# Latent attention with its scores computed twice: row maxima first, then probabilities as keys x queries

## What is computed

```python
x = x + _attn_ref(_layernorm(x), W_dq, W_uq, W_dkv, W_uk, W_uv, W_o)
# inside: nh = 16 heads of hs = 8
c_kv = x @ W_dkv.T
q = x @ W_dq.T @ W_uq.T
q_lat = einsum('bqhd,hdl->bhql', q, k_eff)
attn = einsum('bhql,bkl->bhqk', q_lat, c_kv) / sqrt(hs)
attn = softmax(where(causal, attn, -inf), axis=-1)
y_lat = einsum('bhqk,bkl->bhql', attn, c_kv)
y = einsum('bhql,hld->bqhd', y_lat, v_eff)
```

## Time and profile before

| | |
|---|---|
| median of 3 runs | 2167.96 us |
| the profiled execution's own time | 2170.55 us |
| its span, first to last instruction | 2168.7 us |
| mean granted TensorE clock | 0.955 of 2.4 GHz |
| TensorE (PE) busy | 1785.8 us, 82% |
| its weight loads (PEld) busy | 1079.9 us, 50% |
| DVE (VectorE) busy | 1488.3 us, 69% |
| ACT (ScalarE) busy | 1112.0 us, 51% |
| POOL (GpSimd) busy | 905.7 us, 42% |
| attention stage, first score to last addition | 882.4 to 1341.4 us |

### The profile page before, as it was taken

One profiled execution on the slowest core, in us unless ns is written; L12 is line 12 of the kernel. 1 busy time (PEld: TensorE's weight loads), 2 busy tenths in 40 slices (PEclk: granted clock), 3 DMA queues, 4 the chain that ended last, 5 costly groups with the idle time before them and its releaser, 6 DMA issues. The chain is left out here.

```text
span 2168.7 us, 50695 instructions
## 1 busy us (share of the span) xinstructions
PE 1785.8 (82%) x20074; PEld 1079.9 (50%) x20074; DVE 1488.3 (69%) x2281; ACT 1112.0 (51%) x2070; POOL 905.7 (42%) x624
## 2 busy tenths in 40 slices
PE   1578888888888886899999997578888888888885
PEld 1344444555555543566666664344454455555543
DVE  2567777677666753688888886567777677766752
ACT  1134444454544542688888886234444454544542
POOL 2445544555445540332233321445544555445530
PEclk9889999999999998899999998689999999999998
DMA  4234434544455441000000000334344544355441
GB/s 140 37 58 71 69 62 76 77 80 69 71 79 81 73 68 36 1 1 2 1 2 1 2 1 1 37 63 72 63 71 70 81 75 74 66 85 84 84 72 40
DMA packets 66076, 119.03 MB, mean 55 GB/s; under 512 B 13183, under 2 KB 23603, under 8 KB 63667
## 3 DMA queue, kind: packets, MB, share of 16 engines
q1 hardware_dynamic: 65843, 115.79, 31.8%
HBM read 49.55 MB, written 3.28 MB: 24 GB/s over the span
## 5 line engine op out<-in xcount | busy, mean ns | idle before, releaser
L786 DVE SCALAR_TENSOR_TENSOR TP<-bank,cols,tab 128x1024 f32<-128x1024 f32 x256 | 318.4, 1274 | 51.5 <-PE bank L450 42.5
L946 POOL TENSOR_TENSOR QK<-QK,RB 128x1024 f32<-128x1024 f32 x128 | 302.4, 2363 | 118.6 <-DMA RB<-RN 118.6
L940 POOL TENSOR_TENSOR QK<-TP 128x512 f32<-128x512 f32 x128 | 164.9, 1289 | 327.4 <-DVE TP L786 291.3
L1205 ACT ACTIVATE PL<-bank,NM 128x384 f32<-128x384 f32 (+3 forms) x512 | 255.7, 539 | 15.8 <-DVE NM L1286 13.0
L1286 DVE TENSOR_REDUCE NM<-bank 128x1 f32<-128x384 f32 (+3 forms) x352 | 217.9, 635 | 35.6 <-PE bank L1119 31.7
L809 DVE TRANSPOSE_TENSOR_REDUCE MX<-bank 128x16 f32<-128x512 f32 x256 | 160.2, 681 | 118.3 <-PE bank L487 118.3
L642 ACT ACTIVATE SQ<-bank 128x512 f32<-128x512 f32 x128 | 76.5, 598 | 275.7 <-PE bank L450 275.5
L1128 PE MATMUL bank<-cst,PL 128*128 128x128 f32 x1280 | 199.7, 275 | 3.6 <-DVE PTL L1295 1.4
L827 DVE TENSOR_TENSOR OT<-bank,OT 128x512 f32<-128x512 f32 x128 | 85.3, 687 | 160.9 <-DMA OT<-sums_d 146.9
L1114 PE MATMUL bank<-KL,QZL 128*128 128x384 f32 (+3 forms) x512 | 189.8, 422 | 2.3 <-DVE QZL L1242 2.3
L648 ACT ACTIVATE SQ<-bank 128x512 f32<-128x512 f32 x128 | 76.5, 598 | 201.2 <-DVE TP L786 201.2
(11 more groups left out here) (169 smaller groups left out, 3655.8 us busy)
## 6 DMA issues: line engine op xcount, KB each, us to landing
RB<-RN SPq DMA_DIRECT2D x512, 64.0 KB, 4.0
OT<-sums_d SPq DMA_DIRECT2D x128, 256.0 KB, 4.0
V<-V SPq DMA_DIRECT2D x32, 512.0 KB, 6.0
V<-V SPq DMA_DIRECT2D x32, 384.0 KB, 7.1
RB<-vars_d SPq DMA_DIRECT2D x32, 256.0 KB, 3.2
X<-in_L_attn_x SPq DMA_DIRECT2D x8, 256.0 KB, 4.6
out<-X SPq DMA_DIRECT2D x8, 256.0 KB, 4.7
wqkv_raw<-in_L_ffn_wqkv SPq DMA_DIRECT2D x1, 1536.0 KB
```

Of the source, the lines that this page charges most:

```text
L786: nc.vector.scalar_tensor_tensor(out=TP[:, o:o + 2, :], in0=BK[4 + z][:, :].unsqueeze(1).to_broadcast([P, 2, T]), scalar=q, in1=tab[:, e, ...
L940: nc.gpsimd.tensor_tensor(QK[:, m, 0, :], TP[:, 2, :], TP[:, 1, :], ALU.subtract)
L946: nc.gpsimd.tensor_tensor(QK[:, m, :, :], QK[:, m, :, :], RB[:, m, :].unsqueeze(1).to_broadcast([P, 2, T]), ALU.mult).then_inc(S["nr_ok"], 1)
L1205: last = nc.scalar.activation(PL[:, m % PRING, h * N:(h + 1) * N], BK[m % SRING][:, h * N:(h + 1) * N], ACT.Exp, bias=NM[:, m % SRING, h:h ...
```

## The change

It touches the attention stage and, in the setup, the layout of folded weights and constants. A group now has 6 units in place of 11, each a pair of heads in a pair of banks (1024 columns): `FILLS` puts query block 3 in the first, blocks 2 and 0 in the second, block 1 in the third; two units each, for the two pairs of heads. Every head has 32 rows of its own: 8 high, 8 low and again 8 values, a row (24) for the maximum, and zeros; for the two heads of a pair the products use different 32-row strips.

Per step m TensorE issues the first pass for unit m: masks, then scores, queries x keys (`scores`). DVE takes maxima over both banks (`maxima`). When a group is through, TensorE turns the maxima (`turn_max`, 4 transpositions into bank 7) and DVE adds them to the queries' row 24 (`add_max`), against which the keys have a one. Eight steps later the second pass computes keys x queries with the maximum already in it, and the masks behind it (`scores_t`); ACT takes one exp over both banks straight into `PTL` (`softmax_exp`). PV then needs no transposed copy; it comes in three steps, with key blocks 1 and 3 together. The output copy goes to ACT, the splitting of queries and keys to POOL, and queries and keys are prepared two groups ahead. Both passes share a ring of three bank pairs; the turned output goes back into bank 6.

```diff
-                PT_LAG, PV_LAG, YT_LAG = 3, 5, 11
-                EV_LAG, OT_LAG, Y_LAG = 3, 8, 11
-                SRING, PRING = 4, 4
-                B_PT, B_O, B_PREP = (4, 5), 6, 7
+                FILLS = [((3, 0),), ((2, 0), (0, 3 * P)), ((1, 0),)]
+                DIAG = [(3 * P, T), (2 * P, T), (P, 2 * P)]
+                FILLS_T = [((0, 0),), ((3, 0), (1, P)), ((2, 0),)]
+                DIAG_T = [(0, P), (0, 2 * P), (0, P)]
+                WIDTH_T = [T, T, 2 * P]
+                UN = 2 * len(FILLS)
+                RING = 3
+                AHEAD, QRING, KRING = 2, 3, 4
+                C_AT, Q_AT, K_AT = 1, 2, 4
+                XT_AT, V_AT, VL_AT = (AHEAD, 0), (AHEAD, 5), (AHEAD + 1, 0)
+                T_LAG = UN + 2
+                PV_LAG = {0: T_LAG + 4, 1: T_LAG + 5, 3: T_LAG + 5, 2: T_LAG + 7}
+                YT_LAG, Y_LAG = T_LAG + 8, T_LAG + 9
...
+                        def scores(m):
...
+                            for e in range(2):
+                                nc.tensor.matmul(pair[:, e, lo:hi], identb[:, :],
+                                                 causalb[:, :].unsqueeze(1).to_broadcast([P, (hi - lo) // P, P]),
+                                                 start=True, stop=False, skip_group_check=True)
+                            for i, o in FILLS[f]:
+                                N = (i + 1) * P
+                                for e in range(2):
+                                    rows = slice(32 * (h0 + e), 32 * (h0 + e) + 32)
+                                    last = nc.tensor.matmul(pair[:, e, o:o + N],
+                                                            QS[rows, G % QRING, i * P:(i + 1) * P].bitcast(F32R),
+                                                            KS[rows, G % KRING, 0:N].bitcast(F32R),
+                                                            start=False, stop=True, skip_group_check=True)
+                            last.then_inc(S["s_in"], 1)
...
+                        def turn_max(G):
+                            pe.wait_ge(S["nm_ok"], UN * (G + 1))
+                            claim(B_PREP, "qc_ok", G + 1)
+                            for i in range(NT):
+                                last = pe.transpose(BK[B_PREP][:, i * P:(i + 1) * P], NM[:, G % 2, i, :], ident)
+                            last.then_inc(S["c_in"], 1)
...
+                        def scores_t(m):
...
+                            for j, o in FILLS_T[f]:
+                                N = T - j * P
+                                for e in range(2):
+                                    rows = slice(32 * (h0 + e), 32 * (h0 + e) + 32)
+                                    nc.tensor.matmul(pair[:, e, o:o + N],
+                                                     KS[rows, G % KRING, j * P:(j + 1) * P].bitcast(F32R),
+                                                     QC[rows, G % 2, j * P:T].bitcast(F32R),
+                                                     start=(o == 0), stop=False, skip_group_check=True)
+                            for e in range(2):
+                                last = nc.tensor.matmul(pair[:, e, lo:hi], identb[:, :],
+                                                        causaltb[:, :].unsqueeze(1).to_broadcast([P, (hi - lo) // P, P]),
+                                                        start=False, stop=True, skip_group_check=True)
+                            last.then_inc(S["t_in"], 1)
...
                         for m in range(STEPS):
                             G, r = divmod(m, UN)
+                            if r == C_AT and 1 <= G <= ALLG:
+                                turn_max(G - 1)
+                            if batch_at(m, XT_AT):
+                                xt(batch_at(m, XT_AT))
+                            if batch_at(m, V_AT):
+                                values(batch_at(m, V_AT))
+                            if r == Q_AT and G + AHEAD < ALLG:
+                                queries(G + AHEAD)
+                            if r == K_AT and G + AHEAD < ALLG:
+                                keys(G + AHEAD)
                             if m < ALLU:
+                                scores(m)
+                            if 0 <= m - T_LAG < ALLU:
+                                scores_t(m - T_LAG)
+                            for j in PV_LAG:
+                                g = group_at(m, PV_LAG[j])
+                                if g is not None:
+                                    attend(g, j)
+                            g = group_at(m, YT_LAG)
                             if g is not None:
+                                turn_out(g)
...
+                        def softmax_exp(m):
...
+                            nc.scalar.activation(PTL[:, G % 2, h0:h0 + 2, f * T:f * T + WIDTH_T[f]],
+                                                 PAIR[at_t(m) % RING][:, :, 0:WIDTH_T[f]], ACT.Exp).then_inc(S["ex_ok"], 1)
...
+                        def maxima(m):
...
+                            for i, o in FILLS[f]:
+                                last = nc.vector.tensor_reduce(NM[:, G % 2, i, 24 + 32 * h0:57 + 32 * h0:32],
+                                                               PAIR[at(m) % RING][:, :, o:o + (i + 1) * P],
+                                                               AX_X, ALU.max, negate=True)
+                            last.then_inc(S["nm_ok"], 1)
+
+                        def add_max(G):
...
+                            nc.vector.tensor_tensor(QC[:, G % 2, :].bitcast(F32R), BK[B_PREP][:, :], QS[:, G % QRING, :],
+                                                    ALU.add).then_inc(S["qc_ok"], 1)
...
+                        def stack_q(G):
+                            pool.wait_ge(S["rq_ok"], G + 1)
+                            link(nc.gpsimd.tensor_scalar(HI[:, 0, :].bitcast(F32R), RAW[:, 0, :], low_q, None, ALU.mult))
...
+                            nc.gpsimd.tensor_tensor(QS[:, G % QRING, :].bitcast(F32R), RAW[:, 0, :], HI[:, 0, :],
+                                                    ALU.subtract).then_inc(S["qs_ok"], 1)
```

More of the change, by code:

```diff
@@ L49, in shape_constants @@
     causal = np.where(np.arange(P)[None, :] <= np.arange(P)[:, None], 0.0, BIG).astype(np.float32)
-    headsel = row % (LG * DG) // DG == np.arange(LG)[None, :]
-    low = [-1.0 * (row // (LG * DG) >= 2), -1.0 * (row // (LG * DG) % 2)]
+    part = row % 32 // DG
+    split = [part == 2, part == 1, row % 32 == 24]
     hsum = row // 32 == np.arange(32)[None, :] // 8
@@ new lines, in attend @@
+                        def attend(G, j):
+                            pe.wait_ge(S["ex_ok"], UN * G + READY[j])
+                            if j == 0:
+                                pe.wait_ge(S["vl_ok"], G // GROUPS + 1)
+                                if G == 0:
+                                    pe.wait_ge(S["preset"], 1)
+                                claim(B_O, "ot_ok", G + 1)
+                            for q in range(LG):
+                                last = nc.tensor.matmul(BK[B_O][32 * q:32 * q + 32, j * P:T],
+                                                        VL[:, G // GROUPS % 2, j, G % GROUPS * LG + q, :],
+                                                        PTL[:, G % 2, q, AT_T[j]:AT_T[j] + T - j * P],
+                                                        start=(j == 0), stop=(j == 2), skip_group_check=True)
+                            if j == 2:
+                                last.then_inc(S["o_in"], 1)
@@ L1089, in _, with turn_out @@
+                        def turn_out(G):
+                            claim(B_O, "y_ok", G + 1)
+                            for t in range(NT):
+                                last = pe.transpose(BK[B_O][:, t * P:(t + 1) * P], OTL[:, t * P:(t + 1) * P], ident)
+                            last.then_inc(S["y_in"], 1)
                         xt(0)
                         pe.wait_ge(S["fold_in"], 16)
+                        for G in range(AHEAD):
+                            queries(G)
+                            keys(G)
@@ L1180, in _, with turn_out @@
+                        def turn_out(G):
+                            act.wait_ge(S["o_in"], G + 1)
+                            if G >= 1:
+                                act.wait_ge(S["y_in"], G)
+                            nc.scalar.activation(OTL[:, :], BK[B_O][:, :], ACT.Copy).then_inc(S["ot_ok"], 1)
+                        for G in range(AHEAD):
+                            raw_q(G)
+                            raw_k(G)
                         values(0)
-                        high_q(0)
@@ new lines, in _ @@
+                            if batch_at(m, VL_AT):
+                                values(batch_at(m, VL_AT))
+                            g = group_at(m, YT_LAG)
+                            if g is not None:
+                                turn_out(g)
+                            if r == Q_AT + 1 and G + AHEAD < ALLG:
+                                raw_q(G + AHEAD)
```

(10 more changed lines are left out.)

382 lines of the change are left out of this document (147 added, 235 removed).

## The result

The changed kernel took 2151.8 us, median of 10 runs (2141.2 to 2160.2), against 2168.7 for the kernel before, also of 10. The ratio is 0.992, 95% interval 0.9896 to 0.9944: 17 us faster, where 23 were forecast (2145, range 2108 to 2182). The profiled execution took 2160.2, the slowest of the ten, with a span of 2158.4. That is only 10.3 less than the span before: the attention stage is 13.8 shorter (464.6 us from the last instruction of the FFN stage to the last addition, instead of 478.4), what follows it 0.5, and what lies ahead of it 4.0 longer (867.0 instead of 863.0). In the traces of the changed kernel's repetition and variants the stage begins at 860.5 to 869.4, so these 4 us are within what one trace differs from the next; a cost of the new setup isn't separated from it.

What follows compares the result with a forecast made beforehand. TensorE was taken to bound the attention stage: 12.73 us of work plus waits gave 13.4 a group instead of 14.2. With the stage's ends, -23 us from 2168.0 gave 2145, range 2108 to 2182.

Steps and rivals of the forecast that it cites:

- products of both passes, with the exposed load and the way out: Score streams, 2.65 us a group, plus per step an exposed weight load of 0.106 and 0.09 out of strips.
- bf16 loads beside the masks: Masks following strip products: an exposed bf16 weight load of some 0.05 us in each of six steps a group.
- wait for maxima in the fourth step: Fourth step's second-pass product waits 0.2 us for its bank pair, whose maxima on DVE follow the step before.
- a batch's preparation and its waits, a quarter: Per group, a batch's preparation at 0.33 us and its late bank claims at 0.5 us.
- The values' wait: A batch's values wait for the preparation bank behind the keys' copy on ACT: 1.5 us lost.
- the terms given for ACT: ACT's exps and copies per group, put at 7.5 us of 13, so ACT has room.
- these eight steps: Stage start, first pass alone: bound by DVE's 6.5 us of maxima plus their turn and addition; second pass near 895.5.
- the last eight steps and the output: Stage end: second pass alone, bound by ACT, about 9 us, then last PV through the final addition, 3.3.
- the 184 full steps: Middle of the stage, both passes running: 30.67 groups at 13.4 us, 411 us in all.
- Loads hidden in the same strips: Within a step, weight loads hide behind streams in the same rows, so second-pass products pay no further load.
- Rival A: Loads in the same strips are exposed: 10 of 16 pairs pay 0.106 us more, 33 us, so 2178; chance 0.11.
- rival C: Tiling changes cost only 0.09 us in and out, and waits vanish: 2095 to 2116; chance 0.16.

Runs made afterwards that it cites:

- the fills: Two kernels: the changed kernel plus unread matmuls ahead of the first scores (2144.9 us), and also behind the scores of each of the first eight steps (2145.9 us).
- values later: The changed kernel with the next batch's values issued one step later: 2142.6 us, ratio 0.9871 to the kernel before.

## Why the prediction was right, and where its terms were off

**What bounds, and the group.** The mechanism was right: TensorE bounds the stage, its instructions can be priced by distances between starts, and without the 40 transpositions a group got shorter, 13.35 us against the 13.4 of the sum. That the two agree to 0.1 is in part luck. The terms, from a steady group of the changed kernel (12.28) and the excess of the other three over it:

| term, us a group | sum | measured |
|---|---|---|
| products of both passes, with the exposed load and the way out | 3.83 | 3.74 |
| masks and the way in | 2.58 | 2.39 |
| bf16 loads beside the masks | 0.30 | 0 |
| PV, its changes and exposed loads | 3.00 | 2.85 |
| queries and keys | 1.83 | 1.92 |
| eight transpositions | 0.87 | 0.93 |
| wait for maxima in the fourth step | 0.2 | 0.44 |
| a batch's preparation and its waits, a quarter | 0.83 | 1.07 |

Masks, products and PV came out 0.7 cheaper, mostly for loads that aren't exposed; waits, preparation and projections 0.6 dearer. The values' wait was 1.51 for 1.5, but the transposed input and the turn of maxima behind it wait 0.5 and 0.7 us a batch for 0.6 in all. One slip cost nothing: the terms given for ACT add up to 7.8, not 7.5, but ACT doesn't bound.

**The start and the end of the stage.** Here the sum failed. From the FFN stage's end (863.0) to 1318.8 it has 455.8 us; measured are 464.6, 8.8 more. The first score came 1.2 earlier than summed (20.5 us behind the FFN stage's end). From it to the second pass the sum has 10.8; it took 16.0, 5.2 more. I priced these eight steps by DVE's maxima. They ran on a TensorE at 1.2 GHz, which was the bound in them: it was busy for 34.5 of the first 34.6 us. With the clock high at the first score the fills took 12.7 and 11.8 for them, so 3 to 4 of the 5.2 are the clock. The low clock lasted through six more steps, while before it had ended by 887.3. I had the clock in the text only as 0.99 in the main part, and took the start from rows at the low level without asking whether the new work would raise it. What in the new steps keeps it low isn't shown. At the other end, the last eight steps and the output have 12.3 in the sum and took 17.3 (1314.4 to 1331.7), 5.0 more. A fall of the clock is 2.9 of it: the last two turns lie 8.61 apart, and 5.67 in the five traces without such a fall.

**Falls inside the stage.** Nothing in the sum stood for them: 3.0 and 1.5 us in the two groups. Yet the 184 full steps took 410.9 for 411. That is luck as well: the sum charges preparation to every group, and the last groups have none (their turns lie 10.4 and 10.5 apart), which pays for the two falls and for six steps at the low clock. In "values later", without a fall in a group, the stage took 449.9 us, 28 less than before, 7 of them by that edit; so the stage can give nearly the 22.6 of the sum even with its slow start.

**Loads hidden in the same strips.** The reading was right: 0.34 from the first pass's 512 columns to the second's 256 is the stream and the one load exposed by the change of tiling, and the load behind it adds nothing. Rival A didn't come; rival C neither, for a round trip costs 0.28 to 0.30, well over the 0.09 in and 0.09 out. What the reading left out is that in different strips the whole shorter stream goes, not only a load.

**Chances.** The time fell into the forecast's own range (2120 to 2160), faster by more than 0.3%: 17 us for 23.

## What to carry to other kernels

Price an in-order engine by distances between starts, check that the list closes on the kernel before, and only then sum the new one. When two products that don't depend on each other use strips of the array, give them different strips: the shorter one is then free, as long as it doesn't wait for another engine. And look for the one wait of over 1 us in a stream that is otherwise dense: here it cost itself and, in most of the kernels that have it, falls of the clock behind it. Price the first and the last steps of a stage on their own, at the clock that they will run at.

## What the runs showed of the hardware

- Products issued one behind the other in different 32-row strips start 0.01 us apart, two passes and four banks at once (0.43 us instead of 0.54 for 512 and 256 columns).
- A round trip between 128 rows and strips costs 0.28 to 0.30 us, and 0.2 where the strips are followed by PV, which needs a change anyway. 0.09 of the way in appears without any load: a mask of 128 columns holds TensorE 0.056 ahead of another mask and 0.149 ahead of a strip.
- A weight load behind a stream in the same strips was hidden: 256 columns behind 512 added 0.11 to 0.12 us, where 256 columns alone are 0.11.
- TensorE at 1.2 GHz can stay there although it is always busy: 34.5 of 34.6 us with products of 32 rows, masks, transpositions, queries and keys, until 7.6 us behind the first PV product (914.4). In the kernel before, with 128-row products as scores, it had risen 4.9 us after the first.
- The falls of the clock repeat: in both traces of the changed kernel they come 116.0 and 385.7 us behind the clock's fall at the stage's start (867.4 and 869.9).
